# Attention scores of a transformer layer: from three bf16 parts on 96 rows to two float32r parts on 48 rows, two heads on the two halves of the PE array

## The reference, cut to what matters

```python
scores = jnp.einsum('bqhd,bkhd->bhqk', Q, K) / math.sqrt(D_K)
scores = jnp.where(causal, scores, -jnp.inf)
attn = jax.nn.softmax(scores, axis=-1)
out = jnp.einsum('bhqk,bkhd->bqhd', attn, V)
```

## Time and profile before

| | us |
|---|---|
| median of 3 runs | 2898.09 |
| span of the profiled execution | 2894.7 |
| stage A, its last store issued | about 20 to 262 |
| first load of stage B to its first maximum ready | 265.0 to 381.4 |
| one step with S and M blocks (15 of them, 380.4 to 2027.3) | 109.8 |
| the last step, S blocks only, ends | about 2134 |

### The profile page before, as it was taken

How to read it: one execution, slowest core, us unless ns; L and a number is a source line. 1 busy time by engine, 2 the same in 40 slices (tenths; PEclk the granted TensorE clock), 3 DMA queues, 4 the chain that set the end, 5 groups by cost and what they waited for, 6 DMA issues and landing times. The chain is left out here.

```text
span 2894.7 us, 52029 instructions
## 1 busy us (share of the span) xinstructions
PE 2444.6 (84%) x15097; PEld 1180.6 (41%) x15097; DVE 2012.3 (70%) x6011; ACT 1571.8 (54%) x3204; POOL 310.4 (11%) x268
## 2 busy tenths in 40 slices
PE   4882899999999999999999999999878407999940
PEld 2541133333333333333333333333237306999930
DVE  4872998888878888888878888888015615666632
ACT  2551047677667777677667677677742103555410
POOL 2445000000000000000000000000013270000034
PEclk9996579999999999999999999999988658999975
DMA  4778640440440440430421321400035104443338
GB/s 126 243 241 189 188 63 3 67 66 4 67 64 6 65 62 9 66 50 21 66 43 29 66 40 31 65 7 5 7 75 138 36 11 153 137 138 130 123 76 113
DMA packets 247944, 223.62 MB, mean 77 GB/s; under 512 B 87124, under 2 KB 224670, under 8 KB 247568
## 3 DMA queue, kind: packets, MB, share of 16 engines
q1 hardware_dynamic: 236944, 193.80, 29.3%
q0 software_dynamic: 10752, 26.80, 4.4%
HBM read 142.63 MB, written 83.89 MB: 78 GB/s over the span
## 5 line engine op out<-in xcount | busy, mean ns | idle before, releaser
L584 ACT ACTIVATE probs<-s_banks 128x512 f32<-128x512 f32 (+3 forms) x2560 | 1210.5, 541 | 503.1 <-PE s_banks L521 252.9
L626 DVE TENSOR_REDUCE rowmax<-m_banks 128x1 f32<-128x512 f32 x1536 | 998.5, 686 | 149.7 <-PE m_banks L535 141.7
L535 PE MATMUL m_banks<-ks,qs 96*128 96x512 bf16 (+3 forms) x2560 | 922.8, 367 | 91.0 <-DMA vs<-v_scratch 59.9
L521 PE MATMUL s_banks<-qs,ks 99*128 99x512 bf16 (+3 forms) x2560 | 865.5, 351 | 15.0 <-ACT probs L584 12.8
L552 PE MATMUL v_banks<-probs,vs 128*32 128x512 f32 (+3 forms) x5120 | 600.3, 541 | 0.0
L535 PEld LDWEIGHTS m_banks<-ks,qs 96*128 96x128 bf16 x2560 | 249.8, 98 | 773.0 <-DVE rowmax L626 362.9
L623 DVE CUSTOM_DVE_ANT_0 unused<-m_banks,c_maskq 128x512 bf16<-128x512 f32 (+3 forms) x1024 | 486.9, 487 | 108.0 <-issue 105.9
L521 PEld LDWEIGHTS s_banks<-qs,ks 99*128 99x128 bf16 x2560 | 248.3, 98 | 177.6 <-ACT probs L584 80.9
L524 PE MATMUL s_banks<-c_maskk,c_identb 128*128 128x128 bf16 x1024 | 223.8, 221 | 0.0
L734 POOL TENSOR_TENSOR c_xn<-c_xn,c_ob 128x1024 f32<-128x1024 f32 x8 | 18.8, 2350 | 1854.3 <-DMA c_xs<-in_L_attn_x 1854.3
L1257 PE MATMUL e_banks<-w_parts,hid_parts 128*128 128x256 f32 x1536 | 188.0, 284 | 0.0
(11 more groups left out here) (181 smaller groups left out, 1698.2 us busy)
## 6 DMA issues: line engine op xcount, KB each, us to landing
w<-in_L_ffn_fc_w SPq DMA_DIRECT2D x32, 1024.0 KB, 5.3
qs<-q_scratch SPq DMA_DIRECT2D x96, 256.0 KB, 17.4
v_scratch<-vt SPq DMA_DIRECT2D x64, 256.0 KB, 4.0
vs<-v_scratch SPq DMA_DIRECT2D x32, 512.0 KB, 23.0
q_scratch<-parts SPq DMA_DIRECT2D x96, 128.0 KB
k_scratch<-parts SPq DMA_DIRECT2D x96, 128.0 KB
ks<-k_scratch SPq DMA_DIRECT2D x16, 768.0 KB, 7.8
ks<-k_scratch SPq DMA_DIRECT2D x16, 512.0 KB, 10.1
```

The source lines that it names most:

```text
L521: ins = pe.matmul(bank, ks[:, now, h, k * P:(k + 1) * P], qs[:, now, h, q * CH + first:(q + 1) * CH], start=True, stop=not diagonal)
L535: ins = pe.matmul(bank, qs[0:PAIR_ROWS, nxt, h, t * P:(t + 1) * P], ks[0:PAIR_ROWS, nxt, h, c * CH:c * CH + width], start=True, stop=True)
L584: act.activation(probs[:, n % PR, 0:width], s_banks[:, (u * NS + n) % SLOTS, 0:width], ACT.Exp, scale=SCALE).then_inc(p_ready, 1)
L626: dve.tensor_reduce(rowmax[:, h, t, c:c + 1], scores, AX.X, ALU.max).then_inc(m_used, 1)
```

## The change

q and k are kept as two float32r parts (high, and what is left). Three products of 16 rows, high times high and the two cross ones, make 48 rows in place of 96 (50 with the maxima in place of 99). The first head of a pair lies on partitions 0 to 49, the second on 64 to 113, so the two matmuls of a pair stand on the two halves of the array.

- Stage A: ScalarE writes the high part once; VectorE makes the low part straight from the bank in one instruction; GpSimd does nothing. A QK unit's bank is free after VectorE. 16 stores of 256 KB per chunk, of the same kind as before, in place of 24 of 128 KB.
- M: 80 units of two heads, in a ring of 2 pairs of banks (4 banks). One reduction of VectorE takes a pair. The mask is added on TensorE: four matmuls of 64 columns per pair on the diagonal.
- S: 80 pairs per group in the same ring of 3 banks. A pair waits until both its banks are free, and gives one signal for both when it is done (four mask matmuls come before that on the diagonal). The exponentials stay single.
- PV has one bank in place of two, and 16 tiles of probabilities in place of 8. At a chunk's end copy (C), T and division (D) stand in an order of their own, and two PV share one key tile later.
- The maxima go by 8 DMAs in two parts; M units of the group after next that go with the last tiles are 8 of 80. The loads are 10. The ones are brought by 12 DMAs; zeros for a later stage are written later. Four small DMAs make the masks' swapped halves.

```diff
+PARTS = 2
+PAIR_ROWS = 3 * HD
+HALF = P // 2
@@ stage_a, vector: split
-                dve.tensor_tensor(rest[:, slot, :], qf[:, slot, :], parts[:, slot, 0, :], ALU.subtract)
-                dve.tensor_copy(parts[:, slot, 1, :], rest[:, slot, :]).then_inc(mid_ready, 1)
+                    dve.scalar_tensor_tensor(out=parts[:, slot, 1, :], in0=src,
+                                             scalar=const[("qb", "kb")[r // 2]][:, r % 2:r % 2 + 1], in1=high,
+                                             op0=ALU.add, op1=ALU.subtract).then_inc(lo_ready, 1)
@@ group_order
+    for n in range(n_t):
+        order.append(("S", 2 * n))
+        order += units[:1]
+        if n - 4 in ends:
+            order.append(("PV", n - 2))
+        order.append(("S", 2 * n + 1))
+        order += units[1:]
+        if n - 2 in ends:
+            order.append(("T", ends_name(n - 2)))
+        elif n - 3 in ends:
+            order.append(("PV", n - 2))
+        elif n > 0 or carried:
+            order.append(("PV", n - 1))
@@ stage_b
+    MRING, SRING = 2, 3
+        qs = sb("qs", [P, SLOTS, PAIRS, S], F32R)
+        ks = sb("ks", [P, SLOTS, PAIRS, S], F32R)
@@ stage_b, gpsimd
-            pool.memset(ks[PAIR_ROWS:STACK, :, :, :], 1.0).then_inc(ones_set, 1)
+            pool.wait_ge(p_used, AHEAD + 1)
@@ stage_b, tensor
+            def masked(bank, half, mask, first):
+                rows = slice(half * HALF, (half + 1) * HALF)
+                for j in range(2):
+                    whole = mask if j == half else mask + "_swapped"
+                    ins = pe.matmul(bank[:, first + j * HALF:first + (j + 1) * HALF], const[whole][rows, :],
+                                    const["identb"][rows, rows], start=False, stop=j == 1)
+                return ins
-                        pe.wait_ge(p_ready, at(i, u, NS, n + 1))
-                        ins = pe.matmul(bank, ks[:, now, h, k * P:(k + 1) * P],
-                                        qs[:, now, h, q * CH + first:(q + 1) * CH], start=True, stop=not diagonal)
+                        pe.wait_ge(p_ready, at(i, u, NS, 2 * n + 2))
+                        for half in range(2):
+                            rows = slice(half * HALF, half * HALF + STACK)
+                            ins = pe.matmul(pair[half], ks[rows, now, pr, k * P:(k + 1) * P],
+                                            qs[rows, now, pr, q * CH + first:(q + 1) * CH], start=True, stop=not diagonal)
+                        if diagonal:
+                            for half in range(2):
+                                ins = masked(pair[half], half, "later_col", 0)
+                        ins.then_inc(s_ready, 2)
@@ stage_b, vector
-                            dve.tensor_tensor_reduce(unused[:, n % GH, 0:width], scores, const["maskq"][:, CH - width:CH], 1.0, NEG,
-                                                     ALU.add, ALU.max, rowmax[:, h, t, c:c + 1]).then_inc(m_used, 1)
+                        dve.tensor_reduce(rowmax[:, v % SLOTS, 2 * pr:2 * pr + 2, t, c:c + 1], m_banks[:, (v * NM + n) % MRING, :, 0:width],
+                                          AX.X, ALU.max).then_inc(m_used, 1)
```

More of the change, by code:

```diff
@@ L36 @@
 NTILE = T // P
-SPLIT = 3
+PARTS = 2
 NEG = -3.0e38
@@ L211, in _ @@
             chunk(NCH // 2 - 1, 1, False)
-        @block.gpsimd
-        def _(pool):
-            with pool.Fori(0, NCH // 2) as i:
-                for k in range(2 * NQK):
-                    slot = k % RING
-                    pool.wait_ge(mid_ready, i * (2 * NQK) + (k + 1))
-                    pool.tensor_tensor(parts[:, slot, 2, :], rest[:, slot, :], parts[:, slot, 1, :],
-                                       ALU.subtract).then_inc(lo_ready, 1)
         @block.scalar
@@ L247, in chunk @@
                         r = QK.index(k)
-                        out = qf[:, r % RING, :]
+                        out = parts[:, r % RING, 0, :]
                         if r < NQK // 2:
@@ L534, in step @@
                         pe.wait_ge(m_used, at(i, v, NM, n + 1))
-                        ins = pe.matmul(bank, qs[0:PAIR_ROWS, nxt, h, t * P:(t + 1) * P],
-                                        ks[0:PAIR_ROWS, nxt, h, c * CH:c * CH + width], start=True, stop=True)
+                        if what == "E" and n == MRING:
+                            pe.wait_ge(mrows_ready, at(i, u, 1, 2))
+                        diagonal = c == t // TPC
+                        for half in range(2):
+                            rows = slice(half * HALF, half * HALF + PAIR_ROWS)
+                            ins = pe.matmul(bank[:, half, 0:width], qs[rows, nxt, pr, t * P:(t + 1) * P],
+                                            ks[rows, nxt, pr, c * CH:c * CH + width], start=True, stop=not diagonal)
+                        if diagonal:
+                            for half in range(2):
+                                ins = masked(bank[:, half, :], half, "later_row", width - P)
                         ins.then_inc(m_ready, 1)
                     elif what == "N":
-                        bank = m_banks[:, ((u + 1) * NM + NM - 1) % SLOTS, 0:P]
-                        pe.wait_ge(m_used, at(i, u, NM, NM + NM))
+                        if early:
+                            pe.wait_ge(m_used, at(i, u + 2, NM, 1 + MRING))
+                        else:
+                            pe.wait_ge(m_used, at(i, u + 1, NM, NM + MRING))
                         pe.wait_ge(negmax_ready, at(i, u, 1, 2))
-                        pe.transpose(bank, negmax[:, :], const["ident"][:, :]).then_inc(m_ready, 1)
+                        pe.transpose(m_banks[:, 0, 0, 0:P], negmax[:, :], const["ident"][:, :]).then_inc(n_ready, 1)
                     elif what == "PV":
-                        n, v = (n, u) if n >= 0 else (NB - 1, u - 1)
-                        q, k, _ = SCORE_BLOCKS[n * GH]
+                        n, v = (n, u) if n >= 0 else (NT - 1, u - 1)
+                        q, k = KEY_TILES[n]
                         first = max(k - TPC * q, 0) * P
```

262 lines of the change are left out of this document (125 added, 137 removed).

## The result

The changed kernel takes 3079.07 us at the median of four runs (3072.71 to 3080.4), the kernel before beside it 2898.36 (2897.73 to 2901.14): a ratio of 1.0615 (interval 1.06 to 1.063), 6% slower. Forecast were 2884, with a range to 3010. The profiled execution has a span of 3076.8 us for 2894.7, +182.1.

What follows compares the result with a forecast made beforehand. TensorE was taken to bound each step by its columns: 111 us for 109.8. Steps +17, last step +2, stage A -30 and first load -3 made -14: 2881 profiled, 2884 as the runs' median, range 2755 to 3010.

Steps and rivals of the forecast that it cites:

- The halves run at once: S and M matmuls of two heads on the array's halves stream together, 29.9 us a group in place of 59.8.
- Rival 3: The array's halves don't run at once in S and M: +21.8 us a step, 3233 in all; chance 0.08.
- The tie A to B: In each tile the second S pair waits for the first pair's first exponential: 1.07 us start to start, full width.
- rival 2: Steps: TensorE tied more loosely to ScalarE, masks and loads cheap; a step of 103 us, 2764 in all; chance 0.22.
- Weight loads: Loads behind a wait in S and M can't be hidden: 80 pairs at 0.055 us, 4.4 us a group.
- Masks: Diagonal blocks of S and M: four 64-column matmuls taken at 0.16 us, together 10.2 us a group (7.3 to 13.6).
- The last step: The step without M units: 100 us against 98 to 99 before, +2.
- Stage A: Stores of q and k parts: 18.2 us of SyncE a chunk for 23.0, the stage ending at 232 for 262, -30.
- the case that bytes decide: Stage A gains 0 at today's mean DMA rate of 205 GB/s: 2914 in all; as a rival, chance 0.06.
- The first load: Before the first M block, zeros (8.4 MB) no longer run beside the load: -3 us (-8 to +3).
- Maxima alone: The first group of maxima, M without S, is bound by VectorE: 84 us as now, a change of 0.
- Rival 1: Weight loads and masks show in full at each S pair's wait: 0.19 us per pair, 3034 in all; chance 0.18.

Runs made afterwards that it cites:

- e5_before_pair: The kernel before, with two S blocks sharing one wait for two banks and one signal: 3113.1 us, ratio 1.0769.
- e2_ring4: The changed kernel with four PSUM banks for S and three single banks for M in place of two pairs: 3210.5 us, ratio 1.1091.
- e12_last: The changed kernel with four useless matmuls behind the first pair of every tile of the last step alone: 3052.9 us, ratio 1.0523.
- e3_store: The changed kernel with the part outermost in the q and k scratch arrays, so a store's 128 rows have one stride: 3030.1 us, ratio 1.0495.
- e6_bf16: The changed kernel with two bf16 parts in place of two float32r ones, less exact: 2754.8 us, ratio 0.9507.
- e8_order: The changed kernel with both M units of a tile between its two S pairs, not one on either side of the second: 2973.0 us, ratio 1.0261.
- e1_filler: The changed kernel with M matmuls of each tile's first unit issued again where TensorE waits for the first exponential: 3045.8 us, ratio 1.0499.

## Why the prediction was wrong

The profiled execution came out 196 us above the forecast for it (3076.8 for 2881). 94 of them are the steps (+111 for +17), 67 the way to the first maxima (+34 for -33), 31 the last step (+33 for +2), and 4 the stages behind. The prediction made a step 111 us. At full clock it is 109.85, close by luck, as two errors in it cancel. Its parts, in its order:

- **The halves run at once**: right, by the pairs recorded in 0.50 us. Rival 3 is out.
- **The tie A to B**: right as a mechanism, and visible as the wait by which rival 2 would be told. 1.07 was forecast, 1.20 measured, and 1.08 with bf16 in place of float32r.
- **Weight loads**: mis-sized. 0.055 a pair was taken from N; measured were 0.12 behind the wait and 0.11 at the next M unit, 9.9 us a step for 4.4. The rule of the Trainium skill that the prediction set beside it ("TensorE: Matmul & The Clock Gate", LDWEIGHTS, 107 ns for 128 columns) is the one that the trace agrees with. N, a plain float32 transpose of identity weights, was the wrong row to carry to float32r.
- **Masks**: mis-sized the other way, 10.2 for about 5 (0.07 for four where 0.16 was taken). This and the loads are the two errors that cancel.
- **The granted clock**: the step that failed. The prediction priced every term at 2.4 GHz, as the earlier trace rows have it (0.99), and let TensorE stand idle 0.63 us in every tile without asking what the clock does then. The lower clock cost 93 us over the 15 steps: an idle time was costed at its length, and here it cost more. That is no law of every wait: in e5_before_pair the same tie cost its length alone, at 0.99. The Trainium skill ("TensorE: Matmul & The Clock Gate", A second HAM failure mode: psum-queue depth-cycling) tells of a kernel that cycles through PSUM banks, idles briefly between groups of matmuls and swings between the two levels of the clock. By that rule, the trace agrees: 0.92 in the steps, 0.72 in the last one. e5_before_pair, at 0.99, shows that the rule does not tell how far the clock falls. It was the rule that spoke against the change, and the prediction did not weigh it.
- **The last step**: +2 forecast (107 in the measure of the table), 137.6 measured. With a fourth bank, and so without the tie, it is 99.8 (e2_ring4): the tie was priced too low, and the clock beside it at nothing. 14 us are clock by e12_last, about 8 the tiles of 2.68 for 2.40 us (28 x 0.28), and some 9 are not divided further.
- **Stage A**: here another step failed, the 16 part stores at 0.60 us each (the 9.6 in its sum). 0.60 is what 128 KB took; 256 KB took 1.21, so the 19.3 us of stores, 7.8 of v (8 x 0.97) and 1.7 make 28.8 a chunk, and 29.6 were measured. -30 became +37 at the stage's end. Its bound for the case that bytes decide was wrong too: the mean of 205 GB/s mixed v and xn at 300 with parts at 190. With e3_store's layout the first maxima come 37 us before those of the kernel before (343.5 for 380.4), near the -33 forecast. The first load was right: from the last store of v to the first M block 34.1 us before, 29.6 after, -4.5 for -3. Maxima alone, 327.5 to 414.3, take 86.8 for 85.3 us.

Of the sum: +17 forecast for the steps, +18 found at full clock and +93 of clock not forecast; -30 forecast and +37 found for stage A; +2 and +32.6 for the last step. Rival 1 gave 3034 with its place right (loads behind the wait), but its price too high (0.19 a pair for 0.12), the masks and the halves wrong, and no clock in it; none of the cases held 3077.

What stays open: why the clock fell more in this kernel (0.92, TensorE busy 87% of the steps) than in e6_bf16 (0.96, 83%) or e5_before_pair (0.99, 90%). The fillers show that work in the wait brings it back; they don't show which property of the work counts. Nor does the profile show what TensorE stands for in the 3 us stops of every third step, in both kernels. The program's loop takes three groups a turn, so that they belong to its turns is likely, but not shown.

## What to carry to other kernels

A new wait of TensorE is not priced by its idle time alone: read the granted clock of the stretch, and ask what it would be with the engine idle in every tile; steps within one trace that differ only in clock give the price (0.40 us per low us here). An issue cost is a row for one size and one layout: divide by bytes before it is carried to a larger transfer, and look for slices in which the DMA share stands at a half. When matmuls get shorter and banks stay the same, look at which ring's buffers come free last; here filling the wait with work that stood elsewhere (e8_order) brought more than any other single edit that kept the arithmetic.

## What the runs showed of the hardware

- Two matmuls of 50 and 48 rows on the two halves of the array are recorded in 0.50 us together, 0.39 with bf16, against 0.38 for one and 0.60 for two bf16 ones of 99 rows on the whole array (e5_before_pair).
- A float32r load of 128 columns is recorded at 0.19 us, and float32r costs 0.12 behind a wait and 0.11 from pair B to the next M unit over bf16 (e6_bf16), which takes 0.23 there for 0.22 of columns.
- A store of 128 rows of 2 KB whose destination is eight blocks of 16 rows ran at half the DMA share and some 204 GB/s; with one stride the share was nine tenths or more (1.04 by the row's account) and 331 GB/s over 50 to 215:

```profile
50.00:215.00 165.00, 147.72 (x516) 87.86 (x514) 83.69 (x248) 81.46 (x143) 0.00 (x0) 1.00 1.04 331
```

- More work made a stretch faster twice, both times with a higher granted clock: the 15 steps by 38 us (e1_filler, 0.97 for 0.92), the last step by 14 (e12_last, 0.90 for 0.72).
- A wait in each tile came with a clock of 0.92 in the changed kernel and of 0.99 in e5_before_pair, with TensorE recorded busy 87% and 90%.
